# Down projections from high and low parts in a cross-attention and FFN kernel on one core

## What is computed

```python
kv_c = kv @ W_kvc          # kv: the context, (512, 1024); W_kvc: (1024, 256)
q_c = q @ W_dq             # q: layer norm of x, (512, 1024); W_dq: (1024, 384)
q_nope = (q_c @ W_uq)...   # 16 heads of 128
q_rope = (q_c @ W_qr)...   # 16 heads of 64, then rotated
k_nope = (kv_c @ W_uk)...; v = (kv_c @ W_uv)...; k_rope = kv_c @ W_kr
# masked softmax of the scores, times v, times W_o, added to x
```

## Time and profile before

| | |
|---|---|
| median of 3 runs | 3144.21 us (3143.25 to 3147.97) |
| profiled execution, own time | 3145.69 us |
| its span, first to last instruction | 3143.9 us |
| mean granted TensorE clock | 0.985 of full speed |
| busy: PE, DVE, ACT, POOL | 97%, 65%, 48%, 22% |
| moved by DMA | 472.85 MB, mean 150 GB/s |

### The profile page before, as it was taken

One profiled execution on the slowest core, in us unless ns is written; L12 is line 12 of the kernel. 1 busy time (PEld: TensorE's weight loads), 2 busy tenths in 40 slices (PEclk: granted clock), 3 DMA queues, 4 the chain that ended last, 5 costly groups with the idle time before them and its releaser, 6 DMA issues.

```text
span 3143.9 us, 40170 instructions
## 1 busy us (share of the span) xinstructions
PE 3046.5 (97%) x13962; PEld 2380.2 (76%) x13962; DVE 2034.3 (65%) x4402; ACT 1518.9 (48%) x2978; POOL 704.7 (22%) x533
## 2 busy tenths in 40 slices
PE   7999999999999999999999999999999999999985
PEld 4788868887688867888678886888868887688862
DVE  2555637776477756777467773777637776477776
ACT  2665525554354534555355552555525554355453
POOL 6222241111311132111411104111041111311127
PEclk9999999999999999999999999999999999999995
DMA  6654445444544445444454444644345444444431
GB/s 208 202 172 161 164 160 192 145 144 149 177 145 135 141 136 198 135 136 143 161 181 130 141 134 154 205 144 141 121 160 177 140 144 158 157 144 144 139 91 8
DMA packets 173191, 472.85 MB, mean 150 GB/s; under 512 B 36401, under 2 KB 64689, under 8 KB 152385
## 3 DMA queue, kind: packets, MB, share of 16 engines
q1 hardware_dynamic: 167920, 469.41, 45.1%
q0 software_dynamic: 5072, 0.88, 0.6%
HBM read 369.33 MB, written 67.31 MB: 139 GB/s over the span
## 4 chain that ended last, share of the span: by engine, by line
PE 86%; DVE 5%; issue 3%; POOL 2%; DMA 2%; ACT 1%; SPq 0%; DVEq 0%; POOLq 0%; ACTq 0%
PE psC L2060 10%; PE psD L2051 10%; PE psE L2060 9%; PE psA L1982 8%; PE psT L2038 6%; PE psB L1991 5%; PE psA L1951 5%; PE psS L2019 4%; PE psD L2002 4%; PE psS L2025 3%; PE psS L2021 3%; PE psS L2022 3%; PE psS L2020 3%; PE psB L1951 3%; PE psA L1973 2%
## 5 line engine op out<-in xcount | busy, mean ns | idle before, releaser
L1108 ACT ACTIVATE exps_ring<-exps_ring,neg_max 128x512 f32<-128x512 f32 x512 | 370.8, 724 | 421.2 <-DVE neg_max L1432 420.8
L1432 DVE CUSTOM_DVE_ANT_0 exps_ring<-psS,mask 128x512 f32<-128x512 f32 x512 | 352.9, 689 | 290.4 <-PE psS L2025 285.0
L1119 ACT ACTIVATE probsT_hi<-psT 128x512 fp32r<-128x512 f32 x472 | 282.3, 598 | 338.8 <-PE psT L2038 336.9
L1114 ACT ACTIVATE exps_ring<-exps_ring,row_sum_inverse 128x512 f32<-128x512 f32 x512 | 369.6, 722 | 60.9 <-DVE row_sum_inverse L1438 60.9
L1444 DVE TENSOR_TENSOR probsT_lo<-psT,probsT_hi 128x512 fp32r<-128x512 f32 x472 | 323.5, 685 | 54.7 <-ACT probsT_hi L1119 53.3
L2060 PE MATMUL psC<-w_o_pair,attn_hi 128*128 128x512 f32 x1016 | 336.2, 412 | 0.7 <-DVE attn_lo L1450 0.7
L2060 PE MATMUL psE<-w_o_pair,attn_hi 128*128 128x512 f32 x896 | 295.5, 411 | 0.0
L2038 PE MATMUL psT<-ident,exps_ring 128*128 128x128 f32 x1888 | 283.2, 272 | 5.6 <-DVE probsT_lo L1444 4.6
L2038 PEld LDWEIGHTS psT<-ident,exps_ring 128*128 128x128 f32 x1888 | 228.7, 140 | 76.3 <-issue 25.8
L1982 PE MATMUL psA<-q_c_hi,w_uq_ring 128*128 128x512 f32 x768 | 259.0, 391 | 1.9 <-DVE rope_term L1374 1.9
L2019 PE MATMUL psS<-k_hi,q_hi 128*128 128x512 f32 x512 | 203.6, 398 | 5.5 <-DVE q_lo L1409 3.8
(11 more groups left out here) (368 smaller groups left out, 6313.9 us busy)
## 6 DMA issues: line engine op xcount, KB each, us to landing
w_o_pair<-w_o_split SPq DMA_DIRECT2D x112, 1024.0 KB, 5.5
w_uq_ring<-w_uq_split SPq DMA_DIRECT2D x114, 384.0 KB, 3.6
w_uv_quad<-w_uv_split SPq DMA_DIRECT2D x29, 1024.0 KB, 5.0
w_uk_ring<-w_uk_split SPq DMA_DIRECT2D x114, 256.0 KB, 2.7
w_qr_sorted<-w_qr_split SPq DMA_DIRECT2D x29, 768.0 KB, 4.3
x_stage<-in_x_dram SPq DMA_DIRECT2D x32, 512.0 KB, 6.0
x_stage<-in_ctx_dram SPq DMA_DIRECT2D x32, 512.0 KB, 3.9
acc<-in_x_dram SPq DMA_DIRECT2D x32, 512.0 KB, 5.4
```

What stands on the lines that cost most here:

```text
L1108: act.activation(E[:, qt, :], E[:, qt, :], ACT.Exp, scale=-1.0, bias=mx[:, i % 2, qt:qt + 1], accum_out=rs[:, i % 2, qt:qt + 1]).then_inc( ...
L1114: act.activation(E[:, qt, :], E[:, qt, :], ACT.Copy, scale=ri[:, i % 2, qt:qt + 1]).then_inc(s_prob, 1)
L1432: dve.tensor_tensor_reduce(E[:, qt, :], psS[qt % 2][:, :], mask[:, qt, :], -SCALE, BIG, ALU.add, ALU.min, mx[:, i % 2, qt:qt + 1]).then_in ...
```

## The change

In batch 0 nothing changes in the products. While it runs, w_dq and w_kvc are split: ScalarE makes the high parts in 3 and 2 copies, VectorE the low parts in place in 3 and 2 subtractions, and SyncE stores all four to DRAM (`put_dq`, `put_kvc`). The four loads of acc move behind the raw weights. The first `turned` of the kernel waits for the stores, since probsT and values overwrite the rooms.

From batch 1 on, high and low weights are loaded apart. ScalarE's copy of a turned bank goes to xT_hi (an F32R view of xT's room) and counts s_xhi; VectorE subtracts it from the bank (`stage_lo`) and counts freeT. The low rows lie in rooms of the heads that are idle then (q_hi to k_lo, rope_out and rope_hi, and under the values). `down_q` and `down_kv` add three products for each column, in an order by operands. w_kvc's low part and w_kr lie where w_dq's high part was and are loaded behind down_q.

```diff
             def load_dq(b):
-                if not (b == 0):
-                    sp.wait_ge(fullD, pos_av(b - 1, NQ - 1, HQ - 1) + 1)
-                sp.dma_start(wD[:, :, :], wdq_v).then_inc(s_wd[0], 16)
+                if b == 0:
+                    sp.dma_start(wD[:, :, :], wdq_v).then_inc(s_wd[0], 16)
+                    return
+                sp.wait_ge(fullD, pos_av(b - 1, NQ - 1, HQ - 1) + 1)
+                if b == 1:
+                    sp.wait_ge(s_dqs, 32)
+                    sp.wait_ge(s_kvs, 32)
+                sp.dma_start(flat_dq[1].bitcast(F32), dq_dram[0]).then_inc(s_wdh, 16)
+                sp.dma_start(flat_dq[2].bitcast(F32), dq_dram[1]).then_inc(s_wdl, 16)
...
+            def load_kvc_lo(b):
+                sp.wait_ge(fullA, b * AN + 2)
+                sp.wait_ge(fullB, b * BN + 1)
+                sp.dma_start(flat_kv[2].bitcast(F32), kv_dram[1]).then_inc(s_wkl, 16)
+
+            def put_dq():
+                sp.wait_ge(s_dqh, 3)
+                sp.dma_start(dq_dram[0], dq_hi0[:, :].bitcast(F32)).then_inc(s_dqs, 16)
+                sp.wait_ge(s_dql, 3)
+                sp.dma_start(dq_dram[1], flat_dq[2].bitcast(F32)).then_inc(s_dqs, 16)
+
+            def put_kvc():
+                sp.wait_ge(s_kvh, 2)
...
-            sp.wait_ge(s_setup, 10)
-            for t in range(TT):
-                sp.dma_start(acc[:, t, :], x_t[0, t]).then_inc(s_acc, 16)
+            put_dq()
             into(0, 0, 1)
+            put_kvc()
...
             raw_uv(1, uv_raw)
+            sp.wait_ge(s_setup, 10)
+            for t in range(TT):
+                sp.dma_start(acc[:, t, :], x_t[0, t]).then_inc(s_acc, 16)
...
                     load_kvc(b + 1)
-                    load_kr(b + 1)
                     load_xs(b + 1, 6)
                     load_xs(b + 1, 7)
+                    load_kvc_lo(b + 1)
+                    load_kr(b + 1)
...
-                    act.activation(xT[:, 4 * half:4 * half + 4, j * P:(j + 1) * P],
+                    dst, done = (xT, freeT) if b == 0 else (xTh, s_xhi)
+                    act.activation(dst[:, 4 * half:4 * half + 4, j * P:(j + 1) * P],
...
                 act.wait_ge(s_turn, tile_no(b, q, i, qt) + 1)
+                if tile_no(b, q, i, qt) == 0:
+                    act.wait_ge(s_dqs, 32)
+                    act.wait_ge(s_kvs, 32)
...
+            def stage_lo(b, j, ctx_side, half):
+                k = (TT * 2 if ctx_side else 0) + 2 * j + half
+                dve.wait_ge(s_xhi, (b - 1) * TN + k + 1)
+                if b == 1 and k == 1:
+                    dve.wait_ge(s_wo[1], 16 * PAIRS)
+                dve.tensor_tensor(stage_lo_room(half, ctx_side)[:, :, j * P:(j + 1) * P],
+                                  stages[k % 4][:, :].rearrange("p (c n) -> p c n", c=4),
+                                  xTh[:, 4 * half:4 * half + 4, j * P:(j + 1) * P].bitcast(F32),
+                                  ALU.subtract).then_inc(freeT, 1)
+
+            def dq_lo():
+                for n in range(3):
+                    part = slice(n * DQW, (n + 1) * DQW)
+                    dve.wait_ge(s_dqh, n + 1)
+                    dve.tensor_tensor(flat_dq[2][:, part], flat_dq[0][:, part], dq_hi0[:, part].bitcast(F32),
+                                      ALU.subtract).then_inc(s_dql, 1)
...
             def prologue(b, ends=None):
+                if ends is not None:
+                    for j in range(2):
+                        for half in range(2):
+                            stage_lo(b, j, True, half)
                 rope_q(b, 0)
                 if ends is not None:
+                    for j in range(2, TT):
+                        for half in range(2):
+                            stage_lo(b, j, True, half)
                     add_end(ends, TT - 2, 1)
+                else:
+                    dq_lo()
                 kvc_lo(b, 0, psB, freeB)
                 kvc_lo(b, 1, psA, freeA)
                 if ends is not None:
                     add_end(ends, TT - 1, 0)
+                else:
+                    kvw_lo()
...
                     norm_stats(b + 1, 2)
+                    stage_lo(b + 1, 0, False, 0)
                     norm_x(b + 1, 2)
+                    stage_lo(b + 1, 0, False, 1)
                 attended_lo(b, NQ - 1, HQ - 1)
...
+                if not last:
+                    stage_lo(b + 1, 1, False, 0)
+                    add_end(b, 0, 0)
+                    norm_stats(b + 1, 3)
+                    add_end(b, 0, 1)
+                    norm_x(b + 1, 3)
+                    stage_lo(b + 1, 1, False, 1)
+                    add_end(b, 1, 0)
+                    stage_lo(b + 1, 2, False, 0)
+                    add_end(b, 1, 1)
+                    stage_lo(b + 1, 2, False, 1)
+                    stage_lo(b + 1, 3, False, 0)
+                    add_end(b, 2, 0)
+                    stage_lo(b + 1, 3, False, 1)
+                    queries_down(b + 1)
...
+            def down_part(ps, w, col, rows, begin, end):
+                for c in range(DB):
+                    mm_ = pe.matmul(ps[:, :], w[:, c, col * P:(col + 1) * P], rows(c),
+                                    start=begin and c == 0, stop=end and c == DB - 1)
+                return mm_
...
+                for col in range(2):
+                    pe.wait_ge(sides[col][2], sides[col][3])
+                    down_part(sides[col][0], wdqh, col, row_hi, True, False)
                 pe.wait_ge(freeT, b * TN + 2 * TT)
...
+                for col in range(2):
+                    down_part(sides[col][0], wdqh, col, x_lo, False, False)
+                pe.wait_ge(s_wdl, 16 * b)
+                for col in range(2):
+                    down_part(sides[col][0], wdql, col, row_hi, False, True).then_inc(sides[col][1], 1)
+                pe.wait_ge(sides[2][2], sides[2][3])
+                down_part(psA, wdqh, 2, row_hi, True, False)
+                down_part(psA, wdqh, 2, x_lo, False, False)
+                down_part(psA, wdql, 2, row_hi, False, True).then_inc(fullA, 1)
...
```

More of the change, by code:

```diff
@@ L136, in xattn_ffn_kernel @@
         xs = sb("x_stage", [P, 2, D])
+        with ExitStack() as over:
+            xTh = over.enter_context(nc.sbuf_tensor("xT_hi", [P, DB, T], F32R))
         xT = sb("xT", [P, DB, T])
@@ L142, in xattn_ffn_kernel @@
         rt = sb("rope_term", [P, T])
+        with ExitStack() as over:
+            x_lo1 = over.enter_context(nc.sbuf_tensor("x_lo_back", [P, DB // 2, T], F32R))
         rr = sb("rope_out", [P, 2, T])
@@ L151, in xattn_ffn_kernel @@
         mask = sb("mask", [P, TT, T], BF16)
+        with ExitStack() as over:
+            dq_hi0 = over.enter_context(nc.sbuf_tensor("w_dq_hi_first", [P, DB * QC], F32R))
         attn = [sb("attn_hi", [P, HQ, T], F32R), sb("attn_lo", [P, HQ, T], F32R)]
@@ L1722, in body @@
                     norm_stats(b + 1, 2)
+                    stage_lo(b + 1, 0, False, 0)
                     norm_x(b + 1, 2)
+                    stage_lo(b + 1, 0, False, 1)
                 attended_lo(b, NQ - 1, HQ - 1)
-                for t in range(TT):
-                    if t == TT - 1 and not last:
-                        queries_down(b + 1)
-                    if not last and t < TT - 1:
-                        add_end(b, t, 0)
-                    if not last and t < TT - 2:
-                        add_end(b, t, 1)
-                    if t == 0 and not last:
-                        norm_stats(b + 1, 3)
-                        norm_x(b + 1, 3)
+                if not last:
[13 more added lines that the diff above has]
+                    queries_down(b + 1)
                 if not last:
@@ L2085, in down_q @@
             def down_q(b):
[L2086 to L2093 removed]
+                if b == 0:
+                    pe.wait_ge(s_wd[0], 16)
+                    pe.wait_ge(freeT, 2 * TT)
+                    down(psA, fullA, freeA, 0, wD, 0)
+                    down(psB, fullB, freeB, 0, wD, 1)
+                    down(psA, fullA, freeA, 1, wD, 2)
+                    return
@@ new lines, in down_q @@
+                pe.wait_ge(s_wdl, 16 * b)
[5 more added lines that the diff above has]
+                down_part(psA, wdql, 2, row_hi, False, True).then_inc(fullA, 1)
+            def down_kv(b):
+                if b == 0:
+                    pe.wait_ge(s_wd[1], 16)
+                    pe.wait_ge(freeT, 4 * TT)
+                    down(psB, fullB, freeB, 2, wDkv, 0)
+                    down(psA, fullA, freeA, 3, wDkv, 1)
+                    return
+                sides = (psB, fullB, freeB, b * BN + 2), (psA, fullA, freeA, b * AN + 3)
+                pe.wait_ge(s_wkh, 16 * b)
+                pe.wait_ge(s_xhi, (b - 1) * TN + 4 * TT)
+                for col, (ps, full, free, n) in enumerate(sides):
+                    pe.wait_ge(free, n)
+                    down_part(ps, wkvh, col, row_hi, True, False)
+                pe.wait_ge(s_wkl, 16 * b)
+                for col, (ps, full, free, n) in enumerate(sides):
```

(5 more changed lines are left out.)

72 lines of the change are left out of this document (61 added, 11 removed).

## The result

The changed kernel takes 3100.17 us (median of 4 runs, 3097.58 to 3101.09) against 3145.7 (3143.25 to 3147.97) for the kernel before on the same chip: a ratio of 0.9852, 95% interval 0.984 to 0.9865. The forecast was 3100. The profiled execution took 3100.04 us, its span 3098.2.

A forecast was written before the change was run, and what follows sets the result against it. TensorE, busy 97% of the span, was taken as the bound, except in batch 0's chain through GpSimd, SyncE and a weight landing. Seven boundaries gain 53 us, batch 0 costs 9.2: 44 off 3144.2 gives 3100, range 3089 to 3118.

The forecast's parts named there:

- Products: Down projections at each batch boundary: columns fall from 6.87 to 5.46 us, gaining 7.0 us a boundary.
- VectorE's order: Ahead of down_q: earlier statistics of stage tile 3 remove a 1.16 us wait; down_q begins 0.55 us earlier.
- stage_lo hidden: Inside down_q: VectorE finishes the low rows before TensorE needs them, with 1.1 us to spare.
- rival 3: Boundaries: VectorE becomes the bound through exposed stage_lo; 3177 us, slower than before; decides from 6.3 us of waits; chance 0.05.
- Loads: Split weight loads at boundaries: high half lands about when needed, low halves hidden; counted 0, ends 0 and 0.5 us.
- which makes about 7 for 1536: Load of a w_dq half: longer rows would let 1536 KB land in about 7 us.
- Rival 1: Boundaries: w_dq's low half lands after 2 x 9.1 us, costing 2 us each; 3115 us; chance 0.10.
- Batch 0: Where the weights are split: the start-up chain grows by 3.5 + 5.7 = 9.2 us, ends 1 and 12.
- GpSimd's 3.5: Batch 0: VectorE's five 1024-column subtractions slow GpSimd's masks by 3.5 us, from a range of 0 to 5.
- SyncE and the landing, 5.7: Batch 0: w_kvc's stores ahead of raw w_uq in the queue make ScalarE's uq_hi 5.7 us later, ends 1 and 7.
- Rival 2: Batch 0 costs nothing on its chain and the context block's wait goes too; 3090 us; chance 0.08.

The follow-up runs named there:

- e4: Changed kernel without the products of high weights by low rows in batches 1 to 7, stage_lo on one column per block: 3069.83 us, ratio 0.9755.
- e3: Kernel before with only VectorE's new order at a batch's end (statistics of stage tile 3 earlier, add_end ahead of queries_down): 3141.78 us, ratio 0.9987.
- e5: Changed kernel with each of the eight stage_lo subtractions of turned x rows made twice: 3121.13 us, ratio 0.9928.
- e2: Changed kernel with VectorE's five low-weight subtractions in batch 0 cut from 1024 to 128 columns: 3097.14 us, ratio 0.9846.
- e1: Changed kernel with batch 0's two stores of split w_kvc issued before the sixteen stack transfers: 3094.84 us, ratio 0.9847.
- e6: Changed kernel with GpSimd's rope_lo in batch 0 moved between the second and third mask rounds: 3093.98 us, ratio 0.9834.
- e8: e6 plus, at the end of batch 0, the load of the next batch's stage tile 2 ahead of a split w_o store: 3092.01 us, ratio 0.9829.
- e10: e6 plus, in batch 0, VectorE making w_kvc's low part behind rope_k instead of ahead of it: 3092.59 us, ratio 0.9832.
- e7: Kernel before, with only rope_lo in batch 0 moved between the second and third mask rounds: 3142.87 us, ratio 0.9993.
- e9: e4 with the first quad's rope_lo between the second and third mask rounds in every batch: 3050.93 us, ratio 0.97.

## Why the prediction was right

**Products.** 7.0 us a boundary predicted; down_q is 16.35 us for 16.4, and with the measured change of the waits 7.0 closes the distance to 0.01 us. e4 shows the same pitch.

**VectorE's order.** 0.55 predicted. By the waits the term is 0.85, and 0.1 more came from the context block; alone in the old kernel it is 0.4 to 0.7 (e3). It was mis-sized low by 0.3, inside its ends.

**stage_lo hidden.** Right, with 1.8 us of spare for 1.1: I counted eight operations at 0.69 each, and back to back they start every 0.60. e5 shows both the spare and what happens without it; rival 3 needed 6.3 us of such waits, and even the doubled ones expose 2.9.

**Loads.** The step "which makes about 7 for 1536" was wrong. w_dq_hi lands after 8.4 to 10.3 us (median 9.0), no sooner than the unsplit load did. It isn't shown that the longer rows bring nothing, since another 1536 KB are issued 0.4 us behind it, and these land after a median of 13.0. The late high half cost little because the need came just late enough: three boundaries of six waited, 0.8 us in all. Rival 1's two times 9.1 us for the low half were wrong as well: it comes after 13.0 and is asked for after 16.

**Batch 0.** 9.2 predicted, 10.1 measured, by terms that were off both ways. GpSimd's 3.5 was 1.7 for the subtractions (e2) and 1.09 net, because rope_q stretched the masks less than before; the sum had no such credit. SyncE and the landing, 5.7, were 6.3: from the first store's issue to the landing I had 8.5 us and it took 8.72, and 8.5 for 2.6 is 5.9 more and not 5.7. Of this e1 gives back 5.1. The masks started 0.92 later. Over all profiled executions they start at 42.6 to 43.2 without the change and at 43.0 to 44.1 with it, so most of the 0.92 is spread. The clock, 0.85 + 1.1, was no term of mine. The 0.85 follows the 5.28 us of idle, which the change made; the 1.1 doesn't belong to the change (below). So the change's own cost is nearer 8.3 us (1.09 + 6.31 + 0.85), against a gain of 7 x 7.98 = 55.9 and not 53. That the sum came within 1.5 us of the measured 45.5 is in part owed to errors that cancel.

**Rival 2** (batch 0 free) is in its first half what e6 does by an edit. Its sum adds the 3 us of the context block where a wait that goes would take them off. e6, e8 and e10 lie at 3092 to 3094, each run of them under every run of the changed kernel.

**Still open:** what decides whether an idle of 2.3 to 2.9 us brings the clock down. At the first boundary it fell in the changed kernel, e1, e2, e4, e6 and e10 after 2.31 to 2.40 us, and stayed at 1.00 in the kernel before and in e7 after 2.38 and 2.34. That isn't the change: it also fell in e3, which is the kernel before in another order (2.34 us, first row), and stayed in e9, a changed kernel (2.37 us, second row).

```profile
396.00:400.00 4.00, 4.00 (x12) 3.20 (x11) 2.01 (x4) 0.30 (x1) 0.00 (x0) 0.60 1.01 390
```

```profile
396.00:400.00 4.00, 4.00 (x22) 3.39 (x21) 2.01 (x5) 1.09 (x2) 0.00 (x0) 1.00 0.97 362
```

Ahead of the first head in batch 0, 2.75 us left it at 1.00 in the changed kernel, and 2.74 brought it to 0.65 over 4 us in e4.

## What to carry to other kernels

When TensorE is 97% busy, count products first: here a float32 product cost two instructions of 0.43 us, 0.86, and the three F32R products in its place 3 x 0.2275 = 0.68. Then ask whether the engine that prepares the operands finishes before they are asked for: here by 1.8 us. Before a one-time cost is accepted, follow its bytes through the queue that carries the next thing waited for; two stores of 1 MB cost 6.3 us ahead of a raw weight and some 1.2 when issued 14 us earlier. And after a gain ask who is next: here GpSimd's 29.4 us of masks and rope_lo, with 7.0 us left.

## What the runs showed of the hardware

- TensorE's idle can cost twice. After 5.28 us of it the granted clock was 0.52 for 5.9 us, after 3.62 us 0.50 over 4 us (e4). After 2.3 to 2.9 us it fell to between 0.50 and 0.76 over 4 us in most executions and stayed at 1.00 in others at the same place. After 0.91 us (e8) and 1.75 us (e1) it stayed at 1.00.
- VectorE with two SBUF operands and GpSimd slow each other, sometimes in part and sometimes for a whole operation. In the changed kernel 1024 columns took 1.22 to 1.63 us on VectorE, and a GpSimd operation of 1.58 us took 2.62. Beside rope_lo 1024 columns took 3.13 us (e6) and 128 columns 1.94 for 0.29 (e2). With rope_lo early, a GpSimd operation of 1.57 took 3.59.
- A load of 1536 KB landed after 9.1 us (kernel before, rows of 1.5 KB per partition). Two such loads from rows of 12 KB, issued 0.4 us apart, landed after 9.0 and 13.0.
